# Weighted sum of a pair of row tiles on TensorE: one group of products, or two parts with a wait each

## The reference, cut to what matters

```python
def _L1_gnn_ref(H, A, W, a_l, a_r):
    mask = A + jnp.eye(n) > 0
    Wh = (H @ W).reshape(n, N_HEADS, D_K)
    sl = jnp.einsum('nhd,hd->nh', Wh, a_l)
    sr = jnp.einsum('nhd,hd->nh', Wh, a_r)
    e = leaky_relu(sl[:, :, None] + sr.T[None, :, :], negative_slope=0.2)
    e = jnp.where(mask[:, None, :], e, -jnp.inf)
    alpha = jnp.nan_to_num(jax.nn.softmax(e, axis=2), nan=0.0)
    out = jnp.einsum('nhm,mhd->nhd', alpha, Wh).reshape(n, OUT_DIM)
    return jax.nn.elu(out)

h = relu(layernorm(x)); x = x + L0(h, adj)      # first layer
h = relu(layernorm(x)); x = x + L1(h, adj)      # the attention above
```

## Time and profile before

| what | value |
|---|---|
| median of three runs | 1027.8 us |
| the profiled execution | 1028.79 us |
| its span | 1027.0 us |
| TensorE matmul busy | 734.3 us (72%) |
| VectorE busy | 733.8 us (71%) |
| ScalarE busy | 344.9 us (34%) |
| GpSimd busy | 362.2 us (35%) |
| mean granted TensorE clock | 0.899 |

### The profile page before, as it was taken

One profiled execution on the slowest core, in us unless ns is written; L12 is line 12 of the kernel. 1 busy time (PEld: TensorE's weight loads), 2 busy tenths in 40 slices (PEclk: granted clock), 3 DMA queues, 4 the chain that ended last, 5 costly groups with the idle time before them and its releaser, 6 DMA issues.

```text
span 1027.0 us, 14091 instructions
## 1 busy us (share of the span) xinstructions
PE 734.3 (72%) x3473; PEld 485.7 (47%) x3474; DVE 733.8 (71%) x2968; ACT 344.9 (34%) x1225; POOL 362.2 (35%) x430
## 2 busy tenths in 40 slices
PE   1267867878677887767777777876557777777775
PEld 1034544545444455444444454544445555555554
DVE  6667776767767677776867777677358878777785
ACT  1024343333434334343433434333413333232332
POOL 0022323232322323232322323223276655555650
PEclk9988999989999889988989899888669899888998
DMA  9999999999999999999999999991234445444541
GB/s 301 416 421 418 422 422 421 422 422 422 424 420 423 418 422 410 414 417 411 405 398 419 404 422 406 409 415 39 86 89 132 126 126 134 125 126 129 133 127 42
DMA packets 68467, 321.98 MB, mean 314 GB/s; under 512 B 13743, under 2 KB 47628, under 8 KB 52000
## 3 DMA queue, kind: packets, MB, share of 16 engines
q1 hardware_dynamic: 44160, 293.88, 70.9%
q0 software_dynamic: 13824, 17.44, 7.0%
q10 hardware_dynamic: 10400, 9.74, 2.8%
HBM read 308.25 MB, written 17.07 MB: 317 GB/s over the span
## 4 chain that ended last, share of the span: by engine, by line
DMA 57%; PE 29%; DVE 8%; SPq 2%; issue 2%; POOL 0%; ACT 0%; ACTq 0%; POOLq 0%; DVEq 0%
DMA big<-in_adj_dram 56%; PE p_pack L694 8%; PE p_u L984 6%; PE p_gT L970 3%; PE p_u L981 3%; DVE big L1107 3%; PE p_hT L957 3%; PE p_u L985 2%; SPq L252 2%; PE p_row L984 2%; DVE p_cnt L1101 1%; DMA x_rows<-in_x_dram 1%; DVE big L1097 1%; PE p_row L981 1%; PE p_row L985 1%
## 5 line engine op out<-in xcount | busy, mean ns | idle before, releaser
L694 PE MATMUL p_pack<-big,pack_w 128*128 128x512 fp8e5 x1024 | 290.2, 432 | 153.7 <-DMA big<-in_adj_dram 140.4
L305 POOL DMA_INDIRECT h0g<-h_table,nbr x192 | 192.2, 1001 | 475.8 <-ACT nbr L542 369.1
L694 PEld LDWEIGHTS p_pack<-big,pack_w 128*128 128x128 fp8e5 x1024 | 100.0, 103 | 293.7 <-issue 208.2
L939 POOL DMA_INDIRECT big<-row_table,lists x160 | 160.6, 1003 | 114.4 <-PE p_u L985 44.2
L376 DVE MAX8 tops<-p_pack 128x8 f32<-128x256 f32 x128 | 48.9, 424 | 130.8 <-PE p_pack L694 130.8
L510 ACT ACTIVATE nbr<-keys 128x1 uint32<-128x1 f32 x64 | 13.0, 203 | 352.5 <-DVE keys L411 352.5
L681 PE MATMUL p_row<-w_gat_and_heads,big 128*128 128x264 f32 x256 | 69.6, 396 | 0.6 <-ACT rows L586 0.6
L657 PE MATMUL p_u<-wselfT,big 128*128 128x256 f32 x256 | 69.4, 396 | 0.0
L981 PE MATMUL p_u<-big,ident 128*128 128x512 f32 x48 | 29.5, 699 | 50.3 <-DVE big L1107 50.3
L984 PE MATMUL p_u<-big 128*128 128x256 f32 x192 | 63.4, 491 | 0.0
L570 ACT ACTIVATE big<-x_rows,nm,rs 128x256 f32<-128x256 f32 x64 | 38.4, 600 | 62.3 <-DVE nm L482 61.3
(11 more groups left out here) (156 smaller groups left out, 1434.3 us busy)
## 6 DMA issues: line engine op xcount, KB each, us to landing
big<-in_adj_dram SPq DMA_DIRECT2D x128, 2048.0 KB, 18.3
row_table<-rows ACTq DMA_DIRECT2D x64, 132.0 KB, 9.5
big<-row_table SPq DMA_DIRECT2D x32, 264.0 KB, 3.2
x_rows<-in_x_dram SPq DMA_DIRECT2D x8, 1024.0 KB, 12.8
out_dram<-big SPq DMA_DIRECT2D x32, 256.0 KB, 3.3
h0g<-h_table,nbr POOLq DMA_INDIRECT x192, 6.2
big<-row_table,lists POOLq DMA_INDIRECT x160
big<-in_L_gnn_w_self_dram ACTq DMA_DIRECT2D x1, 256.0 KB, 5.0
```

Source lines behind the costliest of these rows:

```text
L305: nc.gpsimd.indirect_dma_start(out=h0g[r][:, j:j + 1], out_offset=None, in_=h0_dram[:, :], in_offset=bass.IndirectOffsetOnAxis(ap=nbr[r][: ...
L694: last = nc.tensor.matmul(p_pack[:], pack_w[:, block_no, :], low_bytes(n % HALVES)[:, i, :], start=(block_no == 0), stop=(block_no == BLOC ...
L939: nc.gpsimd.indirect_dma_start(out=dst, out_offset=None, in_=row_dram[:, :], in_offset=bass.IndirectOffsetOnAxis(ap=lists[r][:, n:n + 1], ...
```

## The change

`mix` becomes two functions, `mix_direct` and `mix_edges`. The first waits only for `weigh_direct` (through a semaphore of its own, `direct_weighed`) and does both products with `ident`. The second waits for `weigh_extra` (now alone in raising `weighed`) and does the four products with the listed rows, of which the last raises `mixed`. Both are listed with lag 1, behind `spread`. The number of products and their shapes are the same.

```diff
-            def mix(k, r):
+            def mix_direct(k, r):
                 t = pair_no(k, r)
-                pe.wait_ge(weighed, (t + 1) * 2)
+                pe.wait_ge(direct_weighed, t + 1)
                 if later_pair(k):
                     pe.wait_ge(added, t - RING2 + 1)
                 both = p_mix[r][:].rearrange("p (a d) -> p a d", a=2)
-                nc.tensor.matmul(both, ident[:], G[r][:, :, 0, 0:D], start=True, stop=False)
+                for j in range(ROWS):
+                    nc.tensor.matmul(both, ident[:], G[r][:, :, j, 0:D], start=(j == 0), stop=False)
+
+            def mix_edges(k, r):
+                pe.wait_ge(weighed, pair_no(k, r) + 1)
+                both = p_mix[r][:].rearrange("p (a d) -> p a d", a=2)
                 for a in range(2):
                     for c in range(CHUNKS):
-                        nc.tensor.matmul(both[:, a], edges_to_rows(r, a, c), E[r][:, a + c, 0:D], start=False, stop=False)
-                last = nc.tensor.matmul(both, ident[:], G[r][:, :, 1, 0:D], start=False, stop=True)
+                        last = nc.tensor.matmul(both[:, a], edges_to_rows(r, a, c), E[r][:, a + c, 0:D], start=False,
+                                                stop=(a == 1 and c == CHUNKS - 1))
                 last.then_inc(mixed, 1)
-            run_pairs(pe, (scatter, 0), (spread, 1), (mix, 1))
+            run_pairs(pe, (scatter, 0), (spread, 1), (mix_direct, 1), (mix_edges, 1))
...
-                nc.vector.tensor_tensor(rows_by_head, rows_by_head, w, ALU.mult).then_inc(weighed, 1)
+                nc.vector.tensor_tensor(rows_by_head, rows_by_head, w, ALU.mult).then_inc(direct_weighed, 1)
```

More of the change, by code:

```diff
@@ L855, in preln_gnn_gat_kernel @@
             sem(n) for n in ("maps_ready", "placed", "scattered", "score_step", "shifted"))
-        exp_done, mix_step, weights_spread, edge_step, weighed = (
-            sem(n) for n in ("exp_done", "mix_step", "weights_spread", "edge_step", "weighed"))
+        exp_done, mix_step, weights_spread, edge_step, weighed, direct_weighed = (
+            sem(n) for n in ("exp_done", "mix_step", "weights_spread", "edge_step", "weighed", "direct_weighed"))
         mixed, low_step, res_ready, added = (sem(n) for n in ("mixed", "low_step", "res_ready", "added"))
```

## The result

The changed kernel takes 970.73 us (median of three runs, 967.82 to 976.91) against 1027.8. The ratio is 0.9456, with a 95% interval of 0.9383 to 0.9529; in a second comparison, with more runs, it is 0.947 (0.9429 to 0.951, median 970.45). The forecast was 974.

A forecast was written before the change was run, and what follows sets the result against it. TensorE and VectorE waiting for each other bound the second stage, no engine being full. 29 x (8.33 - 6.6) = 50.2, plus 2.5 + 0.3 + 1.7, makes 54.7 off 1028.79: 974.1 us, range 968 to 990.

The forecast's parts named there:

- the ring: Second stage, once per pair: TensorE's sum, scatter and spread, then VectorE, then the next sum; 7.53 us, to become 5.81.
- VectorE is late next: Second stage: VectorE's own work per pair then sets the period, 6.52 to 6.68 us, taken as 6.6.
- VectorE lines alone: Expected sign: the second stage's chain of waits shows only VectorE, at 97% or more of the stage.
- The rendezvous: Second stage: the spread ends 0.5 us before VectorE's `select` needs it, so the added wait costs nothing.
- T: Start of a pair's products with the listed rows on TensorE, from which the forecast counts its times.
- It doesn't fall behind: Second stage: GpSimd's five gathers per pair take 6.51 us against a period of 6.6; no cost counted.
- The clock: TensorE's idle of 0.85 us per pair replaces 2.07; no fall once the second stage has begun, where falls cost 23 us.
- Start and end: Second stage: the second sum comes 2.5 us earlier, the last period gains 0.3 and the last sum 1.7.
- B: Second stage: gathers stretch to 1.44 us and GpSimd bounds, period 7.2, 991.5 us, or 983 at half; chance 0.14.
- C: Second stage: TensorE's clock falls as before, or the spread comes too late for VectorE: 990 us; chance 0.11.
- D: TensorE stays at 1.2 GHz through the second stage, period about 10.7 us: slower, 1093 us; chance 0.03.
- E: Nothing gained: `ident` products don't start before `weighed`, or another 8.3 us wait stands behind; 1028 +- 2 us; chance 0.02.

The follow-up runs named there:

- e1: Kernel before, with both `ident` products ahead of the listed rows' four, the one wait on both weighings still ahead of all six: 1028.35 us, ratio 1.0014.
- e3: Changed kernel with only the own rows' `ident` product ahead; the direct rows' product follows the listed ones again: 976.43 us, ratio 0.9503.
- e7: Changed kernel without the gather of the middle block of listed rows and without `take_low`'s VectorE instruction: 955.57 us, ratio 0.9305.
- e9: e7 with ScalarE's cast of the maps one pair earlier (lag 1 instead of 2): 950.88 us, ratio 0.9235.
- e5: Changed kernel without the gather of the middle block of listed rows, four gathers a pair instead of five: 966.9 us, ratio 0.9415.
- e6: Changed kernel without `take_low`'s instruction on VectorE: 968.13 us, ratio 0.9429.
- e8: Changed kernel with the `ident` products ahead of the spread instead of behind it: 1062.98 us, ratio 1.034.
- e2: Kernel before, with two extra, overwritten `ident` products between the spread and the sum's wait, the sum staying whole behind it: 1002.29 us, ratio 0.976.

## Why the prediction was right

The forecast was 974 with a range of 968 to 990; measured were 970.7 and 970.5. Point by point:

1. *The `ident` products leave the ring.* Right. 2.00 was worked out behind `weigh_extra`, 1.99 is measured. e1 shows that it needs the split, e3 that the last product's part is small.
2. *VectorE is late next, 6.52 to 6.68, taken as 6.6.* The mechanism is right; the value taken was 0.09 too high, for the sum stood in the middle where its own lower end was the right one: without a wait VectorE starts each instruction before the end of the one before, at L1057 and L1102 too. These are 29 x 0.09 = 2.6 us of the 3.4 between 974.1 and 970.7. Another 1.0 is in the start of the sum, an execution 1.0 above the median. "VectorE lines alone" was not quite so: the exponential of ScalarE is in the chain, with 0.12 us of VectorE's time.
3. *The rendezvous.* Right, as the changed kernel shows with no idle before `select`. The forecast had the spread at T + 4.0 and the margin at 0.5; e7 has `select` released at T + 4.17, and in the changed kernel it starts at T + 4.44 (858.76, with T at 854.32), so the margin is about 0.27. e7 and e9 show that the scatter waits for the cast, as was said there. I had not said that this makes a ring of its own of 6.22, only 0.3 below the bound.
4. *GpSimd.* That it would be as full as VectorE was right, and that it costs nothing too (e5). "It doesn't fall behind" was a near thing: the gathers start 1.302 apart from 735.25 to 942.37 without a pause, so any gain on VectorE now ends at them (e6).
5. *The clock.* No fall in 29 periods, as forecast. The fall goes with the wait: with 2.1 us of it in each pair the clock falls in some pairs (13 of 29 before, 12 in e1; also in e8), with at most 1.2 in each pair it falls in none (e2, e3, the changed kernel). Which of the pairs with the long wait have the fall is open. In e6, where irregular waits for gathers come on top, the clock is 0.97. The price was well sized: 23 us forecast, 24 measured in e2.
6. *Start and end.* 2.5 + 0.3 + 1.7 forecast, 2.65 + 0.4 + 1.6 measured.

The clock at the start came back as I had it, within half a microsecond: forecast for 760.8, 22.1 behind the first gather of before; the changed kernel's stretch from 757 to 758, 22 to 23 behind its first gather, has 0.63, and the next 1.00.

Of the rivals, B (GpSimd the bound) fell by `place`, which waits for no gather in these periods of the changed kernel, and by e5; it shows its face in e6. C fell by the clock of 1.00. D and E came in none of the nine executions of the changed kernel.

One reading against B was wrong. The gather at 855.97 isn't beside L1123, which ends at 855.06 + 0.69 = 855.75; it is beside L1052, whose inputs are one in PSUM and one in SBUF. So the rows of before didn't speak against contact of the two engines. The changed kernel has the case that was meant: the gather at 857.69 takes 1.00 and L1128 beside it 0.68, neither longer than elsewhere.

The Trainium skill's rule in "GPSIMD Engine Reference", section "1. Specifications", that GpSimd and VectorE contend for SBUF, fits what short instructions show, though in hundredths of a microsecond (below) and not at rival B's size. Of the Trainium skill's rule on the clock in "TensorE: Matmul & The Clock Gate", section "HAM oscillation — how this bites in real kernels", the direction holds, idle brings the fall; waits as long as the 3 to 5 us of its example are not needed here, where 2.1 us are enough.

No experiment points to a correct version that beats the changed kernel. VectorE, the gathers and, 0.3 us below, the cast would all have to give, and e5 to e9 get there only by leaving work out. Each gather here is given one index per partition; whether the three listed blocks could come with fewer instructions was not tried.

## What to carry to other kernels

When the chain of waits goes round between two engines that are each some 70% busy, look at what the second waits for: an accumulation can be begun with the operands that are there, and only the late ones belong behind the late wait. Put the early part behind everything that another engine is waiting for, since one place too early turned 5% faster into 3% slower. And before counting on more, work out the next ring and the next full engine: here three of them lie between 6.2 and 6.51 us.

## What the runs showed of the hardware

- Products that compute nothing made the kernel before 24 us faster, because TensorE's clock stayed at 2.4 GHz (e2).
- A short VectorE instruction with two inputs in SBUF takes longer where GpSimd starts a gather just as it begins. In e5 the gather starts at 852.54 and `shift` takes 0.37 (356 ns in the mean, 300 in the changed kernel):

```profile
852.51 0.37 DVE L1077 TENSOR_TENSOR big<-big 128x136 f32<-128x136 f32 x1
852.54 1.00 POOL L941 DMA_INDIRECT big<-row_table,lists  x1 [0.30 <-issue]
```

  In the changed kernel `mask` and the first of `weights` meet the gathers: 308 and 292 ns in the mean, and 288 and 272 in e5, where they don't. That is 0.04 of the 0.05 us between the period of 6.51 and the 6.46 of the last full period, beside which no gather is left. It also says why e5 has 6.53: `shift` takes 0.056 more, `mask` and `weights` together 0.04 less. That the gather is the cause is read from these meetings; no run moved it alone. The gather can be the longer one too: in e7 the one that starts beside `place` takes 1.17 to 1.19 us in most pairs, the others 1.00. The two engines keep the same phase over more than 20 periods; why they lock so was not tried.
